# Self-attention softmax: the reciprocals of the row sums made on GpSimd instead of VectorE

## The chip, the cores and the metric

The kernel runs on one core of one Trainium2 chip, in one launch. The metric is the device time of one execution in microseconds (us). The kernel before took 3425.3 us, the median of three runs (3423.97, 3425.3 and 3429.12).

## What is computed

The input x is (4, 1024, 512) in float32. A first cross-attention block (16 heads, with a context of 64 rows) and a layer norm are followed by a transformer block: quantised self-attention (16 heads of 32 columns), quantised cross-attention, and a gated feed-forward layer with 2048 hidden columns. The change lies in the self-attention alone. Of the reference:

```python
def _fq(x, delta, zp, n_bits):
    xi = _round_ste(x / delta) + zp
    xq = jnp.clip(xi, 0.0, 2.0 ** n_bits - 1.0)
    return (xq - zp) * delta
...
sim = jnp.einsum('bhid,bhjd->bhij', _fq(q, dq, 128.0, 8), _fq(k, dk, 128.0, 8)) * SCALE
attn = jax.nn.softmax(sim, axis=-1)
out = jnp.einsum('bhij,bhjd->bhid', _fq(attn, dw, 0.0, 8), _fq(v, dv, 128.0, 8))
```

So each row of scores is exponentiated, divided by its sum times the step `dw` of the quantisation, rounded to a whole number, and multiplied with the quantised values.

## The kernel before, in words

The work is cut into 8 chunks of 512 query rows, two for each of the 4 batches. For every batch both chunks go through the first cross-attention (`cross`), then each chunk goes through self-attention (`self_attention`) and the rest (`middle`). The feed-forward steps of a chunk are not a stage of their own: `feed` deals them out, by a plan worked out from counts and not from times, into the slots of the following chunk's stages. They are the "hosted" work below. Every engine runs its own list of instructions in the order written here; semaphores join the lists.

Self-attention of a chunk has 64 units. A unit is one head for 128 query rows: scores of 128 x 1024. It runs in 70 slots, slot s issuing stages of different units:

- TensorE makes the scores of unit s (L2006, L2007) into a pair of PSUM banks. There are two such pairs, so unit s waits until ScalarE has emptied the pair of unit s-2. Then come hosted matrix multiplications (L1722 to L1724), then the eight transposes of unit s-5 (L2018) into PSUM bank 4, which is the only bank for them, and in two slots out of four half of the product with the values (L2032).
- VectorE takes the row maximum of unit s (`mx`, L1603). In even slots it next makes the reciprocals of the two units s-2 and s-1: `den` = sum times `dw` (L1609), and `rec` = 1/`den` (L1611). Then it turns the transposed weights of unit s-5 into bf16 (`w1T`, L1622), which empties bank 4, and does its hosted steps (`gate` L1514, `x` L1477).
- ScalarE scales the maximum (`nb`, L1287) and exponentiates from PSUM into `e` (L1293); the same instruction sums the row, and a second short one writes out the sum into `sum1`. There are 5 buffers `e1`: unit s waits until GpSimd has read unit s-5.
- GpSimd multiplies `e` by `rec`, adds 1024 and writes float16, which rounds the number (`w1b`, L989). It does this for unit s-2, in `scale_unit`. There are 3 buffers `w1b`: unit u waits for the transposes of unit u-3. Hosted steps on GpSimd are `u_lo` (L1008), and in the first chunk that hosts any, `fw_lo` (L996). Ahead of unit 8 it adds a bias row to the residual (`x`, L910). Elsewhere it computes `rstd`, a power with exponent -0.5 of one column (L904), for the layer norms.

The waits that the change touches are these: `wait_emptied(("s1", n, s))` says that `e` and the sum of unit s are written, `rec_ready` that the reciprocals of a pair are, `w1_ready` that GpSimd has written `w1b`, `("p1T", n, u)` filled that the transposes of unit u are done.

Of the kernel before, what the change touches and what calls it, by code (L numbers as in the profile page):

```python
# [9 lines left out]
ALU = mybir.AluOpType  # L10
# [3 lines left out]
P = 128  # L14
# [13 lines left out]
UNITS = HG * NT * 4  # L28
# [231 lines left out]
def build(nc, a, out):  # L260

    ctx = ExitStack()
    with ctx:
        def sb(name, shape, dt=F32):
            return ctx.enter_context(nc.sbuf_tensor(name, shape, dt))

        def sem(name):
            return ctx.enter_context(nc.semaphore(name))

        def signal(name, keys, by=1):  # L270
            return Signal(sem(name), keys, by)
# [24 lines left out]
        delta = sb("delta", [P, 8])  # L296
# [17 lines left out]
        nb1 = sb("nb1", [P, 4])  # L314
        sum1 = sb("sum1", [P, 8])
        den1 = sb("den1", [P, 8])
        rec1 = sb("rec1", [P, 8])
        k2 = sb("k2", [P, HG, 4 * SC], BF16)
        v2 = sb("v2", [P, PAIRS, 2 * DH], BF16)
# [70 lines left out]
        chunks = range(CHUNKS)  # L390
# [61 lines left out]
        units = [(n, u) for n in chunks for u in range(UNITS)]  # L452
        maxed1 = signal("maxed1", units)
        nb_ready = signal("nb_ready", units)
        rec_ready = signal("rec_ready", [(n, g) for n in chunks for g in range(UNITS // 2)])
        w1_ready = signal("w1_ready", units)
        e2_done = signal("e2_done", [(n, t) for n in chunks for t in range(NT)])
# [10 lines left out]
        def bank_of(key):  # L468
            return FILL[key][0]

        def bank(i):
            return psum[:, i, :]

        def wait_filled(eng, key):

            i, n = FILL[key]
            eng.wait_ge(filled[i], n + 1)

        def wait_emptied(eng, key):

            i, n = FILL[key]
            eng.wait_ge(emptied[i], n + 1)
# [389 lines left out]
        def _(pool):  # L872
            pool.memset(ident[:], 0.0).then_inc(ident_ready, 1)
            pool.memset(mhalf[:], -0.5).then_inc(ident_ready, 1)
            pool.wait_ge(ident_ready, 2)
            pool.affine_select(out=ident[:], in_=ident[:], compare_op=ALU.not_equal, fill=1.0, base=0,
                               pattern=[[-1, P]], channel_multiplier=1).then_inc(ident_ready, 1)
# [104 lines left out]

            def scale_unit(n, u):

                pool.wait_ge(rec_ready.sem, rec_ready.at((n, u // 2)))
                if u >= NH:
                    wait_filled(pool, ("p1T", n, u - NH))
                pool.sem_inc(waits_over, 1)
                pool.tensor_scalar(w1b[u % NH][:], e1[u % NE][:], rec1[:, u % 8:u % 8 + 1], HALF,  # L989
                                   ALU.mult, ALU.add).then_inc(w1_ready.sem, 1)  # L990
# [358 lines left out]
        def _(dve):  # L1349
            steps = [0]  # L1350

            def link(ins):

                steps[0] += 1
                ins.then_inc(step, 1)
                return ins

            def landed():

                dve.wait_ge(step, steps[0])  # L1360
# [14 lines left out]
            def emptied_bank(ins, key):  # L1375
                return ins.then_inc(emptied[bank_of(key)], 1)
# [220 lines left out]
            def self_attention(n):  # L1597

                for s in range(S_SLOTS):
                    if s < UNITS:  # L1600
                        wait_filled(dve, ("s1", n, s))
                        i = bank_of(("s1", n, s))
                        dve.tensor_reduce(mx1[:, s % 4:s % 4 + 1], psum[:, i:i + 2, :].rearrange("p i n -> p (i n)"),  # L1603
                                          AX, ALU.max).then_inc(maxed1.sem, 1)
                    if s >= 2 and s % 2 == 0 and s <= UNITS:
                        g = s // 2 - 1
                        at = slice(2 * (g % 4), 2 * (g % 4) + 2)
                        wait_emptied(dve, ("s1", n, 2 * g + 1))
                        link(dve.tensor_scalar(den1[:, at], sum1[:, at], delta[:, 3:4], None, ALU.mult))  # L1609
                        landed()  # L1610
                        dve.reciprocal(rec1[:, at], den1[:, at]).then_inc(rec_ready.sem, 1)  # L1611
                    u = s - LAG_T
                    if 0 <= u < UNITS:
                        key = ("p1T", n, u)
                        wait_filled(dve, key)
                        if u % 4 == 0 and u >= 8:
                            g = u // 4 - 2
                            if g % 4 == 3:
                                wait_filled(dve, ("a1", n, g // 4))
                            else:  # L1620
                                dve.wait_ge(w1T_used.sem, w1T_used.at((n, g)))
                        emptied_bank(dve.tensor_scalar(w1T[u % 8][:].rearrange("p k q -> p (k q)"),  # L1622
                                                       bank(bank_of(key)).bitcast(FP16), -HALF, W_HIGH, ALU.add, ALU.min), key)
                    hg, at = divmod(s - LAG_T - 19, 16)
                    if hg >= 0 and at == 0:
                        weighted_low(n, hg)
                    if n >= 1:
                        feed(n - 1, host_plan(n - 1), first_in_S(n) + s)
                weighted_low(n, HG - 1)
# [517 lines left out]
```

## Time and profile before

| | |
|---|---|
| median of 3 runs | 3425.3 us (3423.97 to 3429.12) |
| the profiled execution's own time | 3415.72 us |
| its span, first to last instruction | 3413.9 us |
| TensorE busy | 2951.5 us, 86% |
| VectorE busy | 2205.9 us, 65% |
| ScalarE busy | 1671.2 us, 49% |
| GpSimd busy | 1515.0 us, 44% |
| mean granted TensorE clock | 0.925 |

Busy times are sums over the span; TensorE's ends are modelled, so its share is no measure of its peak. In the page's list of groups, each row has the line, the engine, the operation with its output and inputs, its shapes and count, then the busy time, the mean duration in ns, and the idle time of the engine just before these instructions with what ended it. In the names of engines PE is TensorE, PEld its weight load, DVE VectorE, ACT ScalarE and POOL GpSimd.

### The profile page before, as it was taken

The page shows a single profiled execution, that of the slowest core. Times are in us where ns is not written, and L with a number is a line of the kernel's source. Part 1 is how long each engine was busy: PE and PEld are TensorE (multiplying, and loading weights), DVE is VectorE, ACT ScalarE, POOL GpSimd, SP SyncE. Part 2 cuts the span into 40 slices and gives each one's busy share as a digit, 9 for nine tenths or more (in the row PEclk, how much of TensorE's full clock was granted, in tenths as well). Part 3 has the DMA queues.
Part 4 walks back from the last instruction along what each step waited for, and adds up shares of the span by engine and source line. Part 5 has one row for each costly group of instructions (what it writes and reads, how often), then busy time and mean ns, then how long its engine had stood idle before and what let it go on. Part 6 is the DMA issues. An engine that isn't in the chain of part 4 may idle for free.

```text
span 3413.9 us, 50797 instructions
## 1 busy us (share of the span) xinstructions
PE 2951.5 (86%) x19712; PEld 2143.4 (63%) x19712; DVE 2205.9 (65%) x3543; ACT 1671.2 (49%) x2690; POOL 1515.0 (44%) x1182
## 2 busy tenths in 40 slices
PE   7677686887899899799889889899988989889999
PEld 6555445556677656566667656656777746656777
DVE  4456695883666596786565597687565588588521
ACT  5332572783333484574433375376333276387321
POOL 3554353663645253454455154354364154355321
PEclk9888657998999899899999999999999989999999
DMA  8653102334444213323453313313453322232444
GB/s 273 222 201 133 56 1 111 127 122 185 156 163 151 81 63 124 130 87 149 133 180 115 117 51 128 130 70 130 145 190 99 142 75 100 95 122 75 169 153 160
DMA packets 199758, 436.40 MB, mean 128 GB/s; under 512 B 94944, under 2 KB 103392, under 8 KB 182368
## 3 DMA queue, kind: packets, MB, share of 16 engines
q1 hardware_dynamic: 199520, 433.15, 35.6%
q8 instruction: 158, 2.59, 0.3%
q14 instruction: 80, 0.66, 0.1%
HBM read 363.38 MB, written 65.54 MB: 126 GB/s over the span
## 4 chain that ended last, share of the span: by engine, by line
PE 54%; DVE 24%; ACT 8%; issue 6%; POOL 4%; DMA 3%; SPq 1%; POOLq 0%; DVEq 0%; ACTq 0%
PE psum L1722 16%; PE psum L1724 14%; PE psum L1723 14%; DVE mx L1603 8%; DVE w1T L1622 4%; PE psum L2018 4%; ACT e L1293 2%; PE psum L2006 2%; DVE den L1609 2%; ACT psum L1180 2%; DVE gate L1514 1%; DMA unsplit<-in_L_xattn_ff_w 1%; ACT ht_hi L1179 1%; POOL w_lo L898 1%; PE psum L2032 1%
## 5 line engine op out<-in xcount | busy, mean ns | idle before, releaser
L989 POOL TENSOR_SCALAR w1b<-e,rec 128x1024 f16<-128x1024 f32 x512 | 574.5, 1122 | 696.3 <-DVE rec L1611 506.2
L1603 DVE TENSOR_REDUCE mx<-psum 128x1 f32<-128x1024 f32 x512 | 621.7, 1215 | 50.0 <-PE psum L2007 50.0
L1293 ACT ACTIVATE e<-psum,nb,scale 128x1024 f32<-128x1024 f32 x512 | 617.5, 1206 | 16.9
L1722 PE MATMUL psum<-h_hi,fw_hi 128*128 128x512 f32 x1024 | 463.3, 452 | 31.6 <-DVE h_lo L1379 10.0
L1723 PE MATMUL psum<-h_lo,fw_hi 128*128 128x512 f32 x1024 | 415.6, 406 | 0.0
L1724 PE MATMUL psum<-h_hi,fw_lo 128*128 128x512 f32 x1024 | 414.6, 405 | 0.0
L1622 DVE TENSOR_SCALAR w1T<-psum 128x1024 bf16<-128x1024 f16 x512 | 348.3, 680 | 92.0 <-PE psum L2018 87.2
L2018 PEld LDWEIGHTS psum<-ident,w1b 128*128 128x128 f16 x4096 | 259.8, 105 | 231.4 <-issue 192.4
L2018 PE MATMUL psum<-ident,w1b 128*128 128x128 f16 x4096 | 350.7, 234 | 61.9 <-DVE w1T L1622 58.7
L904 POOL TENSOR_TENSOR rstd<-ve,mhalf 128x1 f32<-128x1 f32 x128 | 86.9, 679 | 484.9 <-DVE ve L1485 484.9
L1477 DVE TENSOR_TENSOR x<-psum,x 128x512 f32<-128x512 f32 x224 | 152.2, 684 | 226.8 <-PE psum L1724 226.1
L1722 PEld LDWEIGHTS psum<-h_hi,fw_hi 128*128 128x128 f32 x1024 | 198.5, 194 | 152.3 <-issue 98.7
L1287 ACT ACTIVATE nb<-mx,nscale 128x1 f32<-128x1 f32 x512 | 149.8, 293 | 257.8 <-DVE mx L1603 249.1
L1722 PE MATMUL psum<-w_hi,ht_hi 128*128 128x512 f32 x640 | 257.9, 403 | 20.4 <-DVE e L1540 13.9
L1008 POOL TENSOR_TENSOR u_lo<-gate,u_hi 128x512 fp32r<-128x512 f32 x128 | 164.4, 1287 | 203.0 <-ACT u_hi L1218 197.3
L1723 PE MATMUL psum<-w_lo,ht_hi 128*128 128x512 f32 x640 | 251.7, 393 | 0.0
L1724 PE MATMUL psum<-w_hi,ht_lo 128*128 128x512 f32 x640 | 251.5, 393 | 0.0
L1722 PE MATMUL psum<-fw_hi,u_hi 128*128 128x512 f32 x512 | 226.3, 442 | 28.4 <-POOL u_lo L1008 13.7
L898 POOL TENSOR_TENSOR w_lo<-mixed,w_hi 128x512 fp32r<-128x512 f32 x140 | 190.2, 1382 | 130.8 <-ACT w_hi L1187 130.8
L1724 PEld LDWEIGHTS psum<-h_hi,fw_lo 128*128 128x128 f32 x1024 | 200.7, 196 | 46.9
L1125 ACT ACTIVATE qt<-psum,rounder,inv 128x512 f32<-128x512 f32 x128 | 99.9, 780 | 247.4 <-PE psum L1724 244.0
L2007 PE MATMUL psum<-k_odd,q_turned 32*128 32x512 bf16 x512 | 219.7, 430 | 0.0
(180 smaller groups left out, 6114.3 us busy)
## 6 DMA issues: line engine op xcount, KB each, us to landing
fw_hi<-pieces SPq DMA_DIRECT2D x168, 512.0 KB, 3.3
fw_lo<-pieces SPq DMA_DIRECT2D x168, 512.0 KB, 4.3
w_hi<-kept SPq DMA_DIRECT2D x45, 1024.0 KB, 4.9
w_lo<-kept SPq DMA_DIRECT2D x45, 1024.0 KB, 7.2
mixed<-mixed SPq DMA_DIRECT2D x32, 1024.0 KB, 5.1
fbias<-in_fside_Bx16xSxS SPq DMA_DIRECT2D x64, 256.0 KB, 3.0
unsplit<-in_L_xattn_ff_w SPq DMA_DIRECT2D x24, 512.0 KB, 5.1
pieces<-fw_hi SPq DMA_DIRECT2D x24, 512.0 KB, 2.6
```

The source lines that it names most:

```text
L898: pool.tensor_tensor(w_lo[s][:, k, :], w_mixed[s][:, k, :], w_hi[s][:, k, :].bitcast(F32), ALU.subtract).then_inc(block_lo_done.sem, 1)
L989: pool.tensor_scalar(w1b[u % NH][:], e1[u % NE][:], rec1[:, u % 8:u % 8 + 1], HALF, ALU.mult, ALU.add).then_inc(w1_ready.sem, 1)
L1008: pool.tensor_tensor(u_lo[:, m, :], gate[:, m, :], u_hi[:, m, :].bitcast(F32), ALU.subtract).then_inc(u_lo_done.sem, 1)
L1293: act.activation(e1[s % NE][:], psum[:, i:i + 2, :].rearrange("p i n -> p (i n)"), ACT.Exp, bias=nb1[:, s % 4:s % 4 + 1], scale=scale[:, 0:1],
L1477: return emptied_bank(dve.tensor_tensor(xt, bank(bank_of(key)), xt, ALU.add), key)
L1603: dve.tensor_reduce(mx1[:, s % 4:s % 4 + 1], psum[:, i:i + 2, :].rearrange("p i n -> p (i n)"), AX, ALU.max).then_inc(maxed1.sem, 1)
L1622: emptied_bank(dve.tensor_scalar(w1T[u % 8][:].rearrange("p k q -> p (k q)"), bank(bank_of(key)).bitcast(FP16), -HALF, W_HIGH, ALU.add, AL ...
L1722: pe.matmul(o, s_hi, m_hi, start=first, stop=False)
L1723: pe.matmul(o, s_hi, m_lo, start=False, stop=False)
L1724: return pe.matmul(o, s_lo, m_hi, start=False, stop=last)
L2007: ins = pe.matmul(bank(i + 1), q1_turned[turned, hg, t * P:t * P + P], k1[1][turned, hg, :], start=True, stop=True)
L2018: ins = pe.transpose(bank(bank_of(key)).bitcast(FP16)[:, k * P:k * P + P], w1b[u % NH][:, k * P:k * P + P], ident16[:])
```

## The change

The two small instructions of a pair of units leave VectorE's list. GpSimd does them at the start of `scale_unit` for the even unit: it waits until the sums of both units are written, multiplies them by `dw`, waits on its own semaphore, raises the result to the power -1 with a second operand `mone` that holds -1, waits again on its own semaphore, and scales. The odd unit of the pair has no wait on `rec_ready` any more. `mone` is filled once at the start.

```diff
+        mone = sb("mone", [P, 2])
...
+        den_ready = signal("den_ready", [(n, g) for n in chunks for g in range(UNITS // 2)])
...
             pool.memset(mhalf[:], -0.5).then_inc(ident_ready, 1)
+            pool.memset(mone[:], -1.0)
...
             def scale_unit(n, u):
 
-                pool.wait_ge(rec_ready.sem, rec_ready.at((n, u // 2)))
+                if u % 2 == 0:
+                    at = slice(u % 8, u % 8 + 2)
+                    wait_emptied(pool, ("s1", n, u + 1))
+                    pool.tensor_scalar(den1[:, at], sum1[:, at], delta[:, 3:4], None, ALU.mult).then_inc(den_ready.sem, 1)
+                    pool.wait_ge(den_ready.sem, den_ready.at((n, u // 2)))
+                    pool.tensor_tensor(rec1[:, at], den1[:, at], mone[:], ALU.pow).then_inc(rec_ready.sem, 1)
+                    pool.wait_ge(rec_ready.sem, rec_ready.at((n, u // 2)))
                 if u >= NH:
                     wait_filled(pool, ("p1T", n, u - NH))
...
-                    if s >= 2 and s % 2 == 0 and s <= UNITS:
-                        g = s // 2 - 1
-                        at = slice(2 * (g % 4), 2 * (g % 4) + 2)
-                        wait_emptied(dve, ("s1", n, 2 * g + 1))
-                        link(dve.tensor_scalar(den1[:, at], sum1[:, at], delta[:, 3:4], None, ALU.mult))
-                        landed()
-                        dve.reciprocal(rec1[:, at], den1[:, at]).then_inc(rec_ready.sem, 1)
```

On VectorE, the list before has these instructions in the middle of a chunk's self-attention; `mx` is the maximum of the unit of the slot, `w1T` belongs to the unit five earlier, and "waits" names the semaphores of an instruction:

```order
L1603 TENSOR_REDUCE mx1<-psum 128x1 [waits filled0]
L1609 TENSOR_SCALAR den1<-sum1,delta 128x2 [waits emptied2]
L1611 RECIPROCAL rec1<-den1 128x2 [waits step]
L1622 TENSOR_SCALAR w1T_1<-psum 128x1024 [waits filled4]
L1603 TENSOR_REDUCE mx1<-psum 128x1 [waits filled2]
L1622 TENSOR_SCALAR w1T_2<-psum 128x1024 [waits filled4]
```

The changed list has at the same place (its lines are numbered differently, L1612 is the maximum and L1624 is `w1T`):

```order
L1612 TENSOR_REDUCE mx1<-psum 128x1 [waits filled0]
L1624 TENSOR_SCALAR w1T_7<-psum 128x1024 [waits filled4]
L1612 TENSOR_REDUCE mx1<-psum 128x1 [waits filled2]
L1624 TENSOR_SCALAR w1T_0<-psum 128x1024 [waits w1T_used,filled4]
```

`den` and `rec` are gone there, and with them VectorE's wait on `emptied2`, that is on ScalarE's sums, which stood between a maximum and `w1T` in every second slot.

On GpSimd, the list before has two scalings for each pair of units, each with a wait on `rec_ready`, and here and there a hosted step:

```order
L989 TENSOR_SCALAR w1b<-e_3,rec 128x1024 [waits rec_ready,filled4]
L1008 TENSOR_TENSOR u_lo<-gate,u_hi 128x512 [waits u_hi_done]
L989 TENSOR_SCALAR w1b<-e_4,rec 128x1024 [waits rec_ready,filled4]
L989 TENSOR_SCALAR w1b<-e_0,rec 128x1024 [waits rec_ready,filled4]
```

The changed list has four instructions for a pair (L998 is the scaling, `filled4` is the wait for the transposes of the unit three earlier):

```order
L991 TENSOR_SCALAR den1<-sum1,delta 128x2 [waits emptied2]
L993 TENSOR_TENSOR rec1<-den1,mone 128x2 [waits den_ready]
L998 TENSOR_SCALAR w1b_2<-e1_0,rec1 128x1024 [waits rec_ready,filled4]
L998 TENSOR_SCALAR w1b_0<-e1_1,rec1 128x1024 [waits filled4]
```

The wait on ScalarE has moved to GpSimd, and two waits on GpSimd's own instructions stand ahead of the first scaling. ScalarE's and TensorE's lists keep their order.

## Rows read from the trace of the kernel before

**Rows 1.** The page's chain that ended last: share of the span by line.
```profile
PE psum L1722 16%; PE psum L1724 14%; PE psum L1723 14%; DVE mx L1603 8%; DVE w1T L1622 4%; PE psum L2018 4%; ACT e L1293 2%; PE psum L2006 2%; DVE den L1609 2%; ACT psum L1180 2%; DVE gate L1514 1%; DMA unsplit<-in_L_xattn_ff_w 1%; ACT ht_hi L1179 1%; POOL w_lo L898 1%; PE psum L2032 1%
```
**Rows 2.** Windows of four chunks' self-attention: busy (count), granted clock, DMA.
```profile
378.00:525.00 147.00, 115.57 (x1152) 67.18 (x1148) 130.21 (x195) 104.59 (x198) 76.32 (x65) 0.51 0.03 12
607.00:785.00 178.00, 158.88 (x1446) 102.76 (x1445) 147.95 (x211) 137.69 (x239) 114.87 (x85) 0.95 0.32 113
1162.00:1316.00 154.00, 137.02 (x1335) 81.24 (x1336) 137.03 (x207) 116.78 (x215) 86.58 (x73) 0.92 0.19 69
1418.00:1591.00 173.00, 158.12 (x1446) 102.31 (x1446) 141.48 (x211) 127.90 (x228) 86.56 (x73) 0.95 0.28 103
```
**Rows 3.** Chain of waits in the windows of Rows 2, in their order, by line.
```profile
by line: DVE mx L1603 26.6%; PE psum L2018 21.4%; DVE w1T L1622 19.3%; PE psum L2006 6.7%; PE psum L2032 5.8%; issue 5.3%; DVE den L1609 5.2%; ACT e L1293 3.5%; DVE rec L1611 3.0%; POOL w1b L989 2.3%; ACT nb L1287 0.8%; PE psum L2007 0.3%
by line: DVE mx L1603 12.9%; issue 12.1%; ACT e L1293 9.4%; PE psum L1722 8.7%; PE psum L2018 6.6%; DVE den L1609 6.5%; PE psum L1723 5.8%; PE psum L1724 5.8%; DVE w1T L1622 5.3%; PE psum L2006 3.9%; DMA unsplit<-in_L_xattn_ff_w 3.1%; ACT n
by line: DVE mx L1603 33.4%; DVE w1T L1622 17.3%; PE psum L1722 6.0%; DVE den L1609 5.8%; PE psum L2018 5.5%; issue 5.3%; ACT e L1293 4.3%; PE psum L2006 4.0%; PE psum L1723 3.3%; PE psum L1724 3.3%; DVE gate L1514 2.7%; DVE rec L1611 1.8%;
by line: PE psum L1722 14.0%; DVE mx L1603 13.0%; PE psum L2018 10.2%; PE psum L1723 9.6%; PE psum L1724 9.6%; issue 8.2%; PE psum L2006 6.5%; DVE w1T L1622 6.4%; ACT e L1293 5.2%; DVE den L1609 3.4%; PE psum L2032 2.9%; ACT gate L1232 2.2%
```
**Rows 4.** Groups by line of the whole span: the instructions moved, and GpSimd's nearest kin.
```profile
L1609 DVE TENSOR_SCALAR den<-sum,delta 128x2 f32<-128x2 f32 x256 | 102.5, 400 | 55.2 <-ACT e L1293 54.9
L1611 DVE RECIPROCAL rec<-den 128x2 f32<-128x2 f32 x256 | 42.4, 166 | 8.8
L989 POOL TENSOR_SCALAR w1b<-e,rec 128x1024 f16<-128x1024 f32 x512 | 574.5, 1122 | 696.3 <-DVE rec L1611 506.2 <-issue 135.1 <-PE psum L2018 50.0
L1052 POOL TENSOR_SCALAR w2b<-e 128x1024 f16<-128x1024 f32 x32 | 33.5, 1047 | 6.7 <-POOL e L1047 6.7
L916 POOL TENSOR_TENSOR x<-x,row_L_xattn_bo 128x1024 f32<-128x1024 f32 x16 | 38.3, 2394 | 0.0
L910 POOL TENSOR_TENSOR x<-x,row_L_xattn_a_bo 128x2048 f32<-128x2048 f32 x16 | 73.1, 4571 | 3.5 <-DVE z L1496 2.8
L874 POOL MEMSET mhalf<- 128x4 f32 x1 | 0.1, 103 | 0.0
```
**Rows 5.** One tile each, `den` and the power `rstd`: durations in ns, min/median/max.
```profile
L1609 DVE TENSOR_SCALAR den<-sum,delta x256: 214/228/4129, 383.0 to 3152.1; 128x2 f32<-128x2 f32 x128
L904 POOL TENSOR_TENSOR rstd<-ve,mhalf x128: 547/779/789, 184.2 to 3262.3; 128x1 f32<-128x1 f32 x128
```
**Rows 6.** Timeline of a stall: start, duration, engine, instruction.
```profile
1185.12 4.54 POOL L910 TENSOR_TENSOR x<-x,row_L_xattn_a_bo 128x2048 f32<-128x2048 f32 x1
...
1186.45 3.23 DVE L1609 TENSOR_SCALAR den<-sum,delta 128x2 f32<-128x2 f32 x1
```
**Rows 7.** Timeline of one pair of units and its transposes, third window of Rows 2.
```profile
1206.99 0.19 ACT L1293 ACTIVATION_READ_ACCUMULATOR e<-psum,nb,scale 128x1 f32 x1
1207.22 0.23 DVE L1609 TENSOR_SCALAR den<-sum,delta 128x2 f32<-128x2 f32 x1
1207.48 0.17 DVE L1611 RECIPROCAL rec<-den 128x2 f32<-128x2 f32 x1
1207.87 1.12 POOL L989 TENSOR_SCALAR w1b<-e,rec 128x1024 f16<-128x1024 f32 x1 [2.06 <-DVE rec L1611]
...
1210.45 1.12 POOL L989 TENSOR_SCALAR w1b<-e,rec 128x1024 f16<-128x1024 f32 x1
1212.53 0.61 PE L2018 MATMUL psum<-ident,w1b 128*128 128x128 f16 x8 [0.17 <-DVE w1T L1622]
1214.53 0.62 PE L2018 MATMUL psum<-ident,w1b 128*128 128x128 f16 x8
```
**Rows 8.** Timeline of `rstd` after its input, without and with VectorE's `z` beside it.
```profile
301.58 0.55 POOL L904 TENSOR_TENSOR rstd<-ve,mhalf 128x1 f32<-128x1 f32 x1 [2.79 <-DVE ve L1485]
303.15 0.54 DVE L1496 TENSOR_SCALAR z<-x,mv,rstd 128x512 f32<-128x512 f32 x1
303.31 0.78 POOL L904 TENSOR_TENSOR rstd<-ve,mhalf 128x1 f32<-128x1 f32 x1 [1.18 <-DVE ve L1485]
```

## The prediction

> **What bounds the kernel now.** I read the page's chain first: TensorE's hosted and projection products carry it, and the two instructions that move are a small part, `den` at 2% [rows 1]. So the answer can't come from whole-span shares. The change acts only in the eight self-attention stages, and I cut the span there. Of the eight, the first (378 to 525 us) and the second (607 to 785) are single cases. The third stands for the third, fifth and seventh ("even" below, 154 us each), the fourth for the fourth, sixth and eighth ("odd", 173 us each), which have the same lengths [rows 2]. The reader should see that no engine is far ahead: in the even stage TensorE and VectorE are both busy 137 of 154 us; in the odd one TensorE is busy 158 of 173 us; GpSimd is at 87 us in both, and at 115 of 178 us in the second stage, where it also splits weight pieces. The first runs at a granted clock of 0.51, TensorE's 1.2 GHz level, with TensorE busy 116 and VectorE 130 of 147 us.
>
> Then I read the chain inside each stage [rows 3]. In the first and the even ones VectorE's maximum and `w1T` lead. In the odd ones TensorE's lines do. That split decides how much a lighter VectorE is worth.
>
> **What is removed.** VectorE loses 256 `den` and 256 `rec`: 102.5 + 42.4 us busy, and 55.2 + 8.8 us idle just before them, 209 us in all [rows 4]. Not all of it is on the path. By the chains, `den` and `rec` hold 5.2 + 3.0 = 8.2% of 147 us, 12.1 us, in the first stage; 5.8 + 1.8 = 7.6% of 154 us, 11.7 us, in an even one; 3.4% of 173 us, 5.9 us, in an odd one, and up to 2.2% more for `rec`, which is not among the twelve lines shown; 6.5% of 178 us, 11.6 us, in the second, with the same remark [rows 3]. Taking 1.5% for the two shares not shown (an estimate, between 0 and their last shown lines), 12 + 14 + 3 x 11.7 + 3 x 8.5 = 87 us is the most that the removal gives, if nothing else is late.
>
> Part of it is a stall. `den` takes 214 to 228 ns but 400 on average, and up to 4129 [rows 4, 5]. The long one of [rows 6] ends at 1189.68, when GpSimd's bias addition ends at 1189.66: `den` is held until GpSimd is through. The mean says that shorter stalls of this kind are common, beside `w1b`. 256 x (400 - 225) ns = 45 us of VectorE's 209 are this. I take it that it can't come back elsewhere on VectorE: `mx`, `w1T` and the hosted steps that remain read PSUM, where `den` had SBUF alone.
>
> **What is added, on GpSimd.** Per pair of units: one `den` of two columns, a wait on its own semaphore, one power of two columns, another such wait.
> - `den` on GpSimd: no such row. Its bounds are a memset of four columns at 0.10 us and the 1024-column scaling at 1.12 [rows 4]. The additions give a fixed part: 4571 - 2394 ns for 1024 columns more leaves about 0.22 us at none. I take 0.25.
> - A wait of GpSimd on itself: `w2b` stands idle 6.7 us before 32 instructions, 0.21 us each [rows 4]. Two of them, 0.42.
> - The power: one column takes 0.55 us at the least [rows 5], and 0.78 when VectorE's `z` (SBUF to SBUF) runs beside it [rows 8]. No such instruction of VectorE runs in self-attention once `den` is gone, so 0.55 is the price of one column. For two, the low end is 0.55 again (a price per instruction), the high end near 0.22 + 2 x 0.33 = 0.88 (the fixed part once, the rest twice), the far end 1.10 (everything twice). I take 0.75, between the first two.
>
> Together 1.42 us a pair, 1.22 to 1.77 with the ends of the power, plus some 0.18 of gaps between the instructions that are not in busy time: 1.6 us.
>
> As latency this is nearly free. Now the first `w1b` of a pair starts 0.69 us after ScalarE has written the second sum (1206.99 + 0.19 to 1207.87), since VectorE comes to `den` only after its maximum; it will start some 1.5 us after. But its transposes come only at 1212.53, 3.5 us after it ends at 1208.99, and those of the second at 1214.53, 3.0 us after 1211.57 [rows 7]. A delay of 0.8 us fits. So it is GpSimd's throughput that counts: what it must do in a stage, one after another. Busy time now, plus 32 x 1.6 us, plus 6 us before the first pair of sums and after the last `w1b` (an estimate from one unit's path in [rows 7]): first stage 76.3 + 51 + 6 = 134 us against 147 now; even 86.6 + 51 + 6 = 144 against 154; odd 144 against 173; second 114.9 + 51 + 6 = 172 against 178 [rows 2].
>
> **The sum.** Each stage gives the smaller of the chain's share and what GpSimd's floor allows, less something for jitter, since a queue at 90% can't be kept full. First: 12 by the chain, 13 by the floor, taken 9. Even: 11.7 by the chain, 10 by the floor, taken 6, three times. Odd: up to 8.5 by the chain, floor far away, but TensorE at 158 of 173 is next and takes back half: 4, three times. Second: 14 by the chain, 6 by the floor, and its DMA waits remain: 1. Total 9 + 18 + 12 + 1 = 40 us. Outside self-attention nothing changes; the one memset at the start is hidden behind the first loads. The profiled execution goes from 3415.7 to about 3376 us. The median of the runs was 9.6 us above that execution, so I predict 3385 us.
>
> Two rules of the Trainium skill bear on this. On the power: the rows show 2.1 ns per column for an addition of two inputs (4571 - 2394 ns over 1024 columns). The page "GPSIMD Engine Reference", section "Elementwise — side-by-side cycle accounting", says that a GpSimd instruction has a dispatch cost in software, and a two-input body then takes about 2.6 cycles a column; by that the second column of the power is nearly free, the power takes 0.55 us, each floor falls by 6 us and the sum would be near -55 us. No row shows two columns. Against the change: the same page, section "Engine selection", advises VectorE for elementwise work because GpSimd is about twice as slow; the rows make it worse than that here, 0.55 against 0.166 us for the reciprocal. By that rule alone the time would rise, which is the last rival below; what weighs against it is that GpSimd idles 67 us in an even stage.
>
> **Rivals.**
> - *GpSimd never limits.* The power costs 0.55, TensorE and ScalarE leave room, and nearly the whole share of the chain comes back: 75 us, 3350 us. For it: GpSimd's floor in an even stage would then be 138 us. Against: TensorE is busy 137 us there, ScalarE 117 with the exponentials in series with the maxima.
> - *The time goes elsewhere.* TensorE, at 89% and 91% in the even and odd stages, is late next, and GpSimd with a power of 0.9 to 1.0 us keeps the first and second stages where they are: 10 us or less comes back, 3415 to 3425 us. For it: TensorE has half of the odd chain. Against: VectorE has over half of the even one.
> - *GpSimd becomes the bound.* One mechanism: in every pair GpSimd needs more than the stage's pair takes, falls behind, uses up the 3 us before the transposes, and from then on TensorE waits for `w1b`. With a power of 1.3 us a pair adds 2.15 us instead of 1.6, a floor 18 us higher: even 162 (+8 each), first 152 (+5), second 190 (+12), odd 162, still under 173: +41 us, 3466 us. It decides from a power of about 1.15 us on, where even 157, first 146 and second 185 cancel the odd stages' gain. For it: nothing shows the power with two columns. Against: 1.3 is more than twice the price of one.
>
> That the change doesn't do what it says is hardly open: the order of both lists shows the two instructions gone from VectorE and present on GpSimd.
>
> **How the numbers follow.** Forecast, between 25 and 60 us gained: 0.52, its own range 3365 to 3400. GpSimd never limits (60 to 85 us): 0.16. Gains of 7 to 25 us, half of the second rival: 0.10. Within 7 us of no change, its other half: 0.09. GpSimd becomes the bound: 0.13. The range goes from 3345, which takes in nearly all of the second case (87 us would be 3338), to 3425, which takes in the small gains and half of the no-change case; outside lie about 0.02 and 0.17. A change of 0.2%, 6.8 us, is about what a measurement can tell from none. Faster: 0.52 + 0.16 + 0.10 = 0.78; same 0.09; slower 0.13.
>
> **What would show it.** The power's mean duration: 0.55 to 0.9 us, else the floors are wrong. The `w1b` rows: idle on VectorE's `rec` gone, and in its place idle on ScalarE's `e`. If TensorE's weight loads of L2018 wait for `w1b` for long in the even stages, GpSimd limits. The self-attention stages should be near 138, 177, 148 and 169 us; the stages between them unchanged. VectorE's busy time should fall by 145 us, and the maximum after `e` should be waiting for TensorE's scores in the even stages. The prediction is wrong if an even stage takes over 154 us, or if the stages shrink and the time does not.

## The result, and the profile after

The changed kernel took 3403.2 us, the median of four runs (3399.72 to 3408.15), against 3425.7 us before (now of four runs too): a ratio of 0.9941, with a 95% interval of 0.9924 to 0.9959. That is a gain of 0.6%, 20 us by the ratio; timed again below, it was 0.9950. Forecast were 40 us. Both executions that were profiled are at the edges of their kernels' scatter, the one before low and this one high, so their spans differ by 7.5 us only, 3413.9 against 3406.4.

The page's chain that ended last, shares of the span by engine and by line:

```profile
PE 60%; DVE 11%; POOL 11%; ACT 7%; issue 6%; DMA 2%; SPq 1%; POOLq 0%; DVEq 0%; ACTq 0%
PE psum L1724 17%; PE psum L1726 15%; PE psum L1725 15%; PE psum L2020 5%; POOL w1b L998 3%; PE psum L2008 3%; DVE mx L1612 2%; ACT e L1302 2%; PE psum L2034 2%; ACT psum L1189 1%; DVE w1T L1624 1%; POOL u_lo L1017 1%; POOL rec L993 1%; DMA fw_lo<-pieces 1%; POOL w_lo L901 1%
```

Where VectorE's maximum had 8% and `den` 2% [rows 1], the maximum (now L1612) has 2%, and GpSimd's scaling (L998) and power (L993) are on the chain instead. The groups of the changed kernel, from the page and from its trace by line, that answer to [rows 4]:

```profile
L1612 DVE TENSOR_REDUCE mx<-psum 128x1 f32<-128x1024 f32 x512 | 623.1, 1218 | 121.2 <-PE psum L2009 121.0
L998 POOL TENSOR_SCALAR w1b<-e,rec 128x1024 f16<-128x1024 f32 x512 | 574.7, 1122 | 138.6 <-PE psum L2020 66.3
L993 POOL TENSOR_TENSOR rec<-den,mone 128x2 f32<-128x2 f32 x256 | 181.8, 710 | 21.4
L991 POOL TENSOR_SCALAR den<-sum,delta 128x2 f32<-128x2 f32 x256 | 75.5, 295 | 275.1 <-ACT e L1302 262.2
```

The power of two columns takes 710 ns (forecast 750), `den` 295 (250). The reader should see the idle times too: GpSimd's 696 us before `w1b` have become 139 there and 275 before `den`, which waits for ScalarE's sums. VectorE now waits for TensorE's scores before the maximum.

The windows of the four stages of [rows 2], in the changed kernel (TensorE, weight load, VectorE, ScalarE, GpSimd busy with counts, then clock and DMA), and the chain inside the third:

```profile
377.00:518.00 141.00, 114.54 (x1136) 66.08 (x1137) 118.73 (x131) 104.58 (x198) 108.44 (x129) 0.51 0.03 12
600.00:784.00 184.00, 161.48 (x1446) 104.19 (x1444) 128.15 (x147) 137.61 (x239) 146.95 (x149) 0.92 0.31 110
1161.00:1313.00 152.00, 138.78 (x1336) 82.40 (x1336) 125.49 (x145) 116.25 (x215) 118.72 (x137) 0.91 0.20 70
1415.00:1586.00 171.00, 156.72 (x1450) 101.98 (x1452) 127.97 (x147) 127.60 (x227) 118.70 (x137) 0.95 0.28 102
```

```profile
by line: POOL w1b L998 17.1%; issue 10.8%; PE psum L2020 10.1%; PE psum L1724 8.9%; PE psum L2008 6.8%; POOL rec L993 6.2%; POOL u_lo L1017 5.1%; PE psum L1725 5.0%; PE psum L1726 4.9%; DVE mx L1612 3.9%; ACT e L1302 3.6%; DVE w1T L1624 3.2
```

In the even stage the maximum and `w1T` led with 33% and 17% [rows 3]. Now GpSimd's scaling, power and `u_lo` lead with 28% together. The second stage got longer, 184 us against 178. GpSimd in the middle of that even stage:

```profile
1195.38 0.29 POOL L991 TENSOR_SCALAR den<-sum,delta 128x2 f32<-128x2 f32 x1
1195.76 0.71 POOL L993 TENSOR_TENSOR rec<-den,mone 128x2 f32<-128x2 f32 x1
1196.70 2.34 POOL L998 TENSOR_SCALAR w1b<-e,rec 128x1024 f16<-128x1024 f32 x2 [0.23 <-POOL rec L993]
1199.13 0.30 POOL L991 TENSOR_SCALAR den<-sum,delta 128x2 f32<-128x2 f32 x1
```

From `den` to `den` it is 3.75 us with nothing hosted between: 0.29, a gap of 0.09, 0.71, a gap of 0.23, twice 1.12 with 0.10 between, 0.09. The added part is 1.32 us with all its gaps; the forecast had 1.42, and 1.6 with gaps in its floors.

The prediction named a sign of GpSimd as a limit: TensorE's weight loads for the transposes waiting for `w1b`. In the even stage, before and then changed (us in total, times, longest):

```profile
PEld psum L2018 <- POOL w1b L989: 6.0, 15, 0.6
PEld psum L2020 <- POOL w1b L998: 13.6, 21, 2.9
```

In the changed kernel 17 of the 64 transposes of this stage start within 0.5 us of the end of their `w1b`; before, none starts sooner than 2.7 us after it. So GpSimd does limit there, part of the time.

The lengths of the self-attention stages in us, from the first maximum to the end of the last `w1T`, read from the timelines of one profile each; "even" and "odd" are means of three stages. The three even stages of one profile can differ by 4 us (146.6 to 150.6 in e1), so a difference of 1 or 2 us between two kernels in this table is within the scatter. A second profile of the kernel before (e13) has 145.6, 177.5, 153.5 and 173.0:

| kernel | first | second | even | odd | time, ratio to before (interval) |
|---|---|---|---|---|---|
| before | 145.8 | 177.4 | 153.4 | 172.1 | 3421.3 to 3424.7 in the four rounds, 1 |
| changed, built again (e1) | 140.1 | 183.4 | 148.9 | 171.0 | 3405.4, 0.9950 (0.9934 to 0.9965) |
| no inversion (e2) | 137.2 | 174.7 | 142.7 | 171.0 | 3379.3, 0.9876 (0.9857 to 0.9895) |
| both engines invert (e3) | 146.0 | 186.9 | 154.8 | 173.9 | 3441.0, 1.0060 (1.0042 to 1.0078) |
| split work (e4) | 139.0 | 176.2 | 143.4 | 171.1 | 3381.0, 0.9879 (0.9862 to 0.9896) |
| changed, bias in four (e5) | 138.3 | 186.7 | 146.9 | 171.3 | 3404.0, 0.9947 (0.9930 to 0.9963) |
| split, bias in four (e6) | 138.3 | 182.9 | 143.1 | 171.2 | 3383.7, 0.9886 (0.9868 to 0.9904) |
| changed, two powers (e7) | 151.9 | 194.4 | 164.7 | 173.5 | 3482.0, 1.0178 (1.0159 to 1.0196) |
| two reciprocals (e8) | 141.0 | 176.5 | 146.0 | 170.5 | 3381.9, 0.9882 (0.9863 to 0.9901) |
| den by columns (e9) | 144.5 | 177.1 | 150.3 | 171.8 | 3407.7, 0.9956 (0.9943 to 0.9970) |
| before, bias in four (e10) | 143.8 | 180.8 | 150.5 | 173.9 | 3421.1, 0.9990 (0.9981 to 0.9998) |
| changed, power alone (e11) | 139.6 | 183.2 | 144.6 | 171.1 | 3391.4, 0.9909 (0.9894 to 0.9925) |
| stall alone (e12) | 144.8 | 179.9 | 153.0 | 171.6 | 3420.0, 0.9997 (0.9986 to 1.0007) |
| ScalarE's den (e15) | 143.0 | 180.1 | 148.4 | 172.0 | 3402.0, 0.9935 (0.9922 to 0.9948) |

### The profile page after: what moved, and what is told of

Read it like the earlier page. It is cut to its first block, busy times and chain, and to the rows that moved or that the text cites. A ratio compares the mean times of both kernels' runs of the same rounds, so it can differ in the third digit from the quotient of the medians.

```text
span 3406.4 us, 50798 instructions
## 1 busy us (share of the span) xinstructions
PE 2956.5 (87%) x19712; PEld 2148.8 (63%) x19712; DVE 2099.8 (62%) x3031; ACT 1669.4 (49%) x2690; POOL 1772.2 (52%) x1695
## 4 chain that ended last, share of the span: by engine, by line
PE 60%; DVE 11%; POOL 11%; ACT 7%; issue 6%; DMA 2%; SPq 1%; POOLq 0%; DVEq 0%; ACTq 0%
PE psum L1724 17%; PE psum L1726 15%; PE psum L1725 15%; PE psum L2020 5%; POOL w1b L998 3%; PE psum L2008 3%; DVE mx L1612 2%; ACT e L1302 2%; PE psum L2034 2%; ACT psum L1189 1%; DVE w1T L1624 1%; POOL u_lo L1017 1%; POOL rec L993 1%; DMA fw_lo<-pieces 1%; POOL w_lo L901 1%
## 5 line engine op out<-in xcount | busy, mean ns | idle before, releaser
L1612 DVE TENSOR_REDUCE mx<-psum 128x1 f32<-128x1024 f32 x512 | 623.1, 1218 | 121.2 <-PE psum L2009 121.0
L998 POOL TENSOR_SCALAR w1b<-e,rec 128x1024 f16<-128x1024 f32 x512 | 574.7, 1122 | 138.6 <-PE psum L2020 66.3
L1624 DVE TENSOR_SCALAR w1T<-psum 128x1024 bf16<-128x1024 f16 x512 | 352.0, 687 | 176.4 <-PE psum L2020 163.6
L1017 POOL TENSOR_TENSOR u_lo<-gate,u_hi 128x512 fp32r<-128x512 f32 x128 | 164.7, 1289 | 202.6 <-ACT u_hi L1227 196.8
```

The source lines that it names most:

```text
L1017: pool.tensor_tensor(u_lo[:, m, :], gate[:, m, :], u_hi[:, m, :].bitcast(F32), ALU.subtract).then_inc(u_lo_done.sem, 1)
```

## The experiments

The first question was where the missing gain is: taken back by GpSimd's added work (theory A), or never there, since TensorE or the score banks are next (theory B). Two more came with the results: theory C, that what GpSimd does per pair counts, wherever its other work stands; and theory D, that the change wins by ending the stalls of `den` beside GpSimd. In the expectations of e9 and e12, "Theory A" beside D means that VectorE's work or its wait counts, and not the stalls. Kernels timed together ran on one chip and share the runs of the kernel before.

**e1, the changed kernel again.** 

> The changed kernel once more, timed beside the kernel before on the same chip. The change gave 0.9941 of the time before; it should stay between 0.990 and 0.997. Both theories expect its second self-attention stage (the one that also splits weight pieces on GpSimd) to be longer than before by some 6 us, as in the first trace. If that stage is back at 177 us, the 6 us were a matter of DMAs.

0.995, and the second stage at 183.4 us: both repeat.

**e2, no inversion.** From the changed kernel, GpSimd's two instructions and their waits are taken out, which leaves out the normalisation; `rec1` is filled with 1.

```diff
-            pool.memset(mone[:], -1.0)
+            pool.memset(rec1[:], 1.0)
...
-                    pool.tensor_scalar(den1[:, at], sum1[:, at], delta[:, 3:4], None, ALU.mult).then_inc(den_ready.sem, 1)
-                    pool.wait_ge(den_ready.sem, den_ready.at((n, u // 2)))
-                    pool.tensor_tensor(rec1[:, at], den1[:, at], mone[:], ALU.pow).then_inc(rec_ready.sem, 1)
-                    pool.wait_ge(rec_ready.sem, rec_ready.at((n, u // 2)))
```

> No sum is inverted at all: neither engine has den or rec, and the factor is a constant 1 written once at the start, so this leaves the normalisation out. Theory A, GpSimd's queue takes back what VectorE gives: the removal alone is worth 60 to 87 us, 3340 to 3365 us, even stages near 140 us. Theory B, TensorE or the ring of score banks is next late whatever GpSimd does: 3390 to 3405 us, even stages near 149 us, as in the changed kernel.

3379 us lies between the two: the removal alone is worth 42 us, and GpSimd's part gives 26 of them back. Theory B fails, since there was more to have than the change got (even stages 142.7 us, not 149); theory A fails in the size of the ceiling. In the even stages it is worth 10.7 us and in the odd ones 1.1, where the chain of waits, here over one odd stage (1397 to 1568 us), remains with TensorE's products:

```profile
by line: PE psum L1720 19.7%; PE psum L2016 15.0%; PE psum L1721 13.3%; PE psum L1722 13.2%; PE psum L2004 9.7%; issue 7.3%; ACT e L1298 5.1%; PE psum L2030 4.5%; DVE mx L1608 3.5%; ACT gate L1237 3.4%; DVE w1T L1620 1.6%; ACT nb L1292 1.4%
```

**e3, both engines.** GpSimd gets the change's two instructions and waits on tiles `den2` and `rec2`, ahead of the old wait.

```diff
+                if u % 2 == 0:
+                    at = slice(u % 8, u % 8 + 2)
+                    wait_emptied(pool, ("s1", n, u + 1))
+                    pool.tensor_scalar(den2[:, at], sum1[:, at], delta[:, 3:4], None, ALU.mult).then_inc(den_ready.sem, 1)
+                    pool.wait_ge(den_ready.sem, den_ready.at((n, u // 2)))
+                    pool.tensor_tensor(rec2[:, at], den2[:, at], mone[:], ALU.pow).then_inc(rec2_ready.sem, 1)
+                    pool.wait_ge(rec2_ready.sem, rec2_ready.at((n, u // 2)))
                 pool.wait_ge(rec_ready.sem, rec_ready.at((n, u // 2)))
```

> The kernel before with GpSimd's two instructions and their two waits added, their result going to a scratch tile; VectorE still makes the reciprocals that are used. Theory A: the added 1.4 to 1.5 us a pair makes the time longer than before, by 20 to 50 us, the even stages 158 to 162 us. Theory B: GpSimd has room, the time is within 10 us of before.

20 us slower, the lower edge of theory A. Half of it is in the second stage (9.5 us); the even ones have 1.4, not 5 to 8. So where VectorE sets the pace, most of GpSimd's added work hides.

**e4, split work.** VectorE inverts the bare sum, GpSimd multiplies by 1/`dw`, which the kernel has in `inv`.

```diff
-                        link(dve.tensor_scalar(den1[:, at], sum1[:, at], delta[:, 3:4], None, ALU.mult))
-                        landed()
-                        dve.reciprocal(rec1[:, at], den1[:, at]).then_inc(rec_ready.sem, 1)
+                        dve.reciprocal(den1[:, at], sum1[:, at]).then_inc(rec_ready.sem, 1)
...
-                pool.wait_ge(rec_ready.sem, rec_ready.at((n, u // 2)))
+                if u % 2 == 0:
+                    at = slice(u % 8, u % 8 + 2)
+                    pool.wait_ge(rec_ready.sem, rec_ready.at((n, u // 2)))
+                    pool.tensor_scalar(rec1[:, at], den1[:, at], inv[:, 3:4], None, ALU.mult).then_inc(scaled_ready.sem, 1)
+                    pool.wait_ge(scaled_ready.sem, scaled_ready.at((n, u // 2)))
```

> VectorE inverts the sum (one instruction of 0.17 us, no den, no step between), GpSimd multiplies the result by the inverse of the quantisation step (0.29 us and one wait on itself). Per pair GpSimd does 3.0 us instead of 3.7. Theory A: the time falls below the changed kernel's, to 3355 to 3385 us, and the second stage is not longer than before. Theory B: 3395 to 3410 us, the same as the changed kernel.

3381 us, the whole ceiling within the scatter, and the softmax is still whole: the version that beats both. GpSimd spends 2.94 us a pair there, as its timeline shows:

```profile
1198.41 0.29 POOL L989 TENSOR_SCALAR rec<-den,inv 128x2 f32<-128x2 f32 x1
1198.93 2.33 POOL L994 TENSOR_SCALAR w1b<-e,rec 128x1024 f16<-128x1024 f32 x2 [0.23 <-POOL rec L989]
1201.35 0.29 POOL L989 TENSOR_SCALAR rec<-den,inv 128x2 f32<-128x2 f32 x1
```

**e5 and e6, the bias addition in four pieces.**

```diff
...
-                    if u == 8:
-                        pool.wait_ge(z_ready.sem, z_ready.at((1, n, NT - 1)))
-                        add_bias(n, "L1_xattn_a1_bo")
+                    if u in (8, 14, 20, 26):
+                        if u == 8:
+                            pool.wait_ge(z_ready.sem, z_ready.at((1, n, NT - 1)))
+                        add_bias_quarter(n, "L1_xattn_a1_bo", (u - 8) // 6)
```

> The changed kernel with GpSimd's bias addition of 4.57 us ahead of unit 8 cut into four of some 1.3 us, ahead of units 8, 14, 20 and 26. Theory A: in the changed kernel that addition puts GpSimd 6 to 8 us behind, and at 3.75 us a pair it catches up only ten pairs later, while TensorE waits for w1b. Then the even stages fall from 147 to 151 us to 142 to 146, and the time to 3385 to 3395 us. Theory C: it is the 3.75 us a pair as such, wherever the addition stands: 3400 to 3410 us.

> The kernel in which VectorE inverts and GpSimd multiplies, with the same four pieces of the bias addition. Both theories expect a small gain over the uncut one, since GpSimd is behind there for six pairs at most: 3370 to 3380 us.

3404 us, no gain in the time: theory A's burst falls as the main cause. By the table the first and even stages are 1.8 and 2.0 us shorter than in e1 and the second 3.3 longer. In the timeline of e1's even stage GpSimd does fall behind at the addition: the first `w1b` of a pair starts 1.4 us after the second sum for the first pairs, 6.2 us after it at the fifth, and still 3.5 at the fifteenth. With four pieces it is 7.0 us at the eighth pair and 4.2 at the fifteenth. In this stretch ScalarE delivers a pair mostly every 3.4 to 4.8 us, so 3.75 us and the hosted work leave little to catch up with. e6 came out at 3384, 4 us above the range expected and no better than e4.

**e7, two powers.**

```diff
+                    pool.tensor_tensor(den2[:, at], den1[:, at], mone[:], ALU.pow)
                     pool.tensor_tensor(rec1[:, at], den1[:, at], mone[:], ALU.pow).then_inc(rec_ready.sem, 1)
```

> The changed kernel with one more power per pair, into a scratch tile, that nobody waits for: 0.71 us more GpSimd work a pair, 4.5 us in all. Theory A, from GpSimd's work per pair, the hosted work and 6 us at the ends: first stage near 153 us, even 164, second 200, odd 172: 3475 to 3490 us. Theory B, that TensorE or the score banks are the bound and GpSimd has room: within 10 us of the changed kernel.

3482 us, stages 152, 194, 165 and 174: theory A's sum holds once GpSimd is plainly the bound. The 0.71 us cost 77 us where e1's 1.32 cost 26.

**e8, two reciprocals.**

```diff
-                        link(dve.tensor_scalar(den1[:, at], sum1[:, at], delta[:, 3:4], None, ALU.mult))
+                        link(dve.reciprocal(den1[:, at], sum1[:, at]))
```

> The kernel before with den as a second reciprocal (the multiplication by the quantisation step is left out, so the weights are not the reference's). VectorE has the same two instructions a pair and the same wait, but none that is held up beside GpSimd. Theory A: the stalls, 45 us of VectorE's time, are a good part of what the change wins: 3395 to 3408 us. Rival: they are hidden behind the score banks, and the instructions themselves are what counts: 3415 to 3422 us.

3382 us, below both expectations. VectorE still does two instructions a pair and still waits for ScalarE before them, and 41 of the 42 us are there:

```profile
L1609 DVE RECIPROCAL den<-sum 128x2 f32<-128x2 f32 x256 | 41.0, 160 | 66.5 <-ACT e L1293 66.2
L1611 DVE RECIPROCAL rec<-den 128x2 f32<-128x2 f32 x256 | 42.5, 166 | 8.8
```

The rows are the groups by line of e8. No `den` there is over 167 ns, against 400 on average before [rows 4]. The kernel has 61 us less of VectorE's time than before, 45 of them stalls.

**e9, `den` by columns.**

```diff
-                        link(dve.tensor_scalar(den1[:, at], sum1[:, at], delta[:, 3:4], None, ALU.mult))
+                        for c in (2 * (g % 4), 2 * (g % 4) + 1):
+                            link(dve.tensor_scalar(den1[:, c:c + 1], sum1[:, c:c + 1], delta[:, 3:4], None, ALU.mult))
```

> The kernel before, with den as two instructions of one column each instead of one of two columns. VectorE has one instruction more a pair (0.15 us, as the one-column ve), nothing moves to GpSimd. Theory D, what the change wins on VectorE is the end of the stalls of den beside GpSimd, and a one-column form is not held up, as ve never is (153 to 155 ns): 3380 to 3392 us, and no den over 0.2 us. Theory A, it is the work taken off VectorE: 3420 to 3435 us, no faster than before.

The tile `den`, durations in ns, min/median/max:

```profile
L1610 DVE TENSOR_SCALAR den<-sum,delta x512: 201/205/217, 382.2 to 3141.3; 128x1 f32<-128x1 f32 x171
```

One column is never held up, as theory D has it: of the 512, 89 start beside a GpSimd instruction that runs on for more than 0.25 us, and none takes over 217 ns. But each takes 205 ns and not the 154 of `ve`. The time is 3408 us, between the two expectations: with one instruction more than before, and all on VectorE, it is 0.4% faster than before. That is 15 us of the 42, though no stall is left. Its mean granted clock over six runs was 0.927, that of the kernel before in the same round 0.922; an estimate below puts 9 of the 15 us beside that.

**e10, before with the bias in four.** The edit of e5 in the kernel before.

> The kernel before, with the bias addition ahead of unit 8 cut into four pieces of some 1.3 us. The one stall of 3 to 4 us a stage becomes short ones. Theory D says that the long stall is a part of the 42 us, 8 of them at 3.3 us: 3403 to 3418 us. If only the many short ones count: 3418 to 3426 us.

`den` falls from 102.5 to 86.4 us, its longest from 4.13 to 1.70 us, and the time by 2 us only, 0.9990. By the table the first and even stages are 2.0 and 2.9 us shorter, where their stalls fell by 1.8 and 2.0 us; the second and odd ones are 3.4 and 1.8 us longer. So the long stall seems to count where VectorE leads, and the cut pieces to cost as much elsewhere; with a scatter of 2 us and more this is not shown.

**e11, the power alone.** GpSimd's `den` and its wait are left out, the power reads `sum1`.

> The changed kernel without its den: GpSimd raises the bare sum to the power -1, so the factor of the quantisation step is left out. GpSimd does 3.4 us a pair instead of 3.75. Theory C, GpSimd's work per pair beyond what the pair leaves it is what takes back the gain: between the kernel with split work (3.0 us a pair, 3381 us) and the changed one (3405): 3386 to 3396 us. If it is the latency of the power alone: 3400 to 3405 us.

3391 us, in the range of theory C: GpSimd's work a pair is what costs. Without 0.38 of the 1.32 us, 14 of the 26 us come back.

**e12, the stall alone.** e2 with this in VectorE's even slots:

```diff
+                    if s >= 2 and s % 2 == 0 and s <= UNITS:
+                        at = slice((s - 2) % 8, (s - 2) % 8 + 2)
+                        link(dve.tensor_scalar(den1[:, at], inv[:, 0:2], delta[:, 3:4], None, ALU.mult))
+                        landed()
```

> The kernel without any inversion of the sums, and with one VectorE instruction of two columns per pair put back at the place of den. It reads constants, waits for nothing of the pair, and its result is not used; only w1T behind it waits until it is written. Theory D: it is held up beside GpSimd as den was, and that alone brings back most of the 42 us: 3402 to 3420 us. Theory A, that the wait on ScalarE and the second instruction matter: 3380 to 3390 us.

3420 us, nearly what before took, from one instruction a pair. Alone it takes 0.22 us; here 57 of the 256 are held up, and the mean is 450 ns. The group, and the long one in the timeline:

```profile
L1612 DVE TENSOR_SCALAR den<-inv,delta 128x2 f32<-128x2 f32 x256 | 115.3, 450 | 0.0
```

```profile
1186.74 4.54 POOL L913 TENSOR_TENSOR x<-x,row_L_xattn_a_bo 128x2048 f32<-128x2048 f32 x1
1187.90 3.40 DVE L1612 TENSOR_SCALAR den<-inv,delta 128x2 f32<-128x2 f32 x1
1191.33 0.69 DVE L1624 TENSOR_SCALAR w1T<-psum 128x1024 bf16<-128x1024 f16 x1
```

GpSimd's addition ends at 1191.28, `den` at 1191.30, and `w1T` comes after it. Nothing is inverted here and VectorE doesn't wait for ScalarE, so neither the reciprocal nor that wait made the 42 us. The stalls are some 58 us here, 13 more than before. e8 has more unstalled work of these instructions, 0.33 us a pair, and is at 3382: what sets e12 apart from it is the stalls.

**e13 and e14, a second profile of before and of split work.**

> The kernel before, one more profile. Its second self-attention stage was 177 us; the kernels that add work to GpSimd had 183 to 187 there. If that is GpSimd's work, it stays within 2 us of 177; if the stage varies by itself with the loads from HBM, it may be anywhere up to 183.

> The kernel with split work, one more profile. Its second stage was 176 us, and 183 with the bias addition cut. The same question: within 2 us of 176 if GpSimd's 3.0 us a pair fit there, up to 183 if the stage varies by itself.

The second stage was 177.5 and 176.6 us, in one run each of 3425.7 and 3378.3 us. It repeats within 0.4 us, so the 6 us more of the changed kernel are no scatter. By e2, which has 174.7, it is GpSimd's two instructions that make them, beside its 12 splits of weight pieces of 2.37 us. How they do isn't settled: e11 has 183.2 and e6 182.9 with less of that work, and e10, e12 and e15 are at 180 to 181 with none of it. The granted clock differs too: in this stage TensorE was at its 1.2 GHz level for 17 us before, 14 in e2 and 31 in e1.

**e15, ScalarE's `den`.** ScalarE multiplies after the second sum of a pair, VectorE inverts.

```diff
...
+                        if s % 2 == 1:
+                            wait_emptied(act, ("s1", n, s))
+                            pair = slice(s % 8 - 1, s % 8 + 1)
+                            act.activation(den1[:, pair], sum1[:, pair], ACT.Copy, scale=delta[:, 3:4]).then_inc(den_ready.sem, 1)
...
-                        wait_emptied(dve, ("s1", n, 2 * g + 1))
-                        link(dve.tensor_scalar(den1[:, at], sum1[:, at], delta[:, 3:4], None, ALU.mult))
-                        landed()
+                        dve.wait_ge(den_ready.sem, den_ready.at((n, g)))
```

> ScalarE multiplies the two sums by the quantisation step (one more instruction of 0.29 us a pair, with a wait on its own sums), VectorE makes the reciprocal, 0.17 us without a stall; GpSimd has nothing added. If what counts is that VectorE spends no more than 0.40 us a pair and is not held up, and ScalarE's time is free: 3378 to 3388 us. If ScalarE's time is on the path through the score banks, 256 x 0.4 us come on top: 3400 to 3430 us.

3402 us. VectorE is as well off as in e4 (a reciprocal of 162 ns, no stall), and still half the gain is gone. What e15 adds beside e4 is ScalarE's 0.30 us a pair and its wait on its own sums, so these count, some 21 us against e4. GpSimd has more room: its added work, gaps included, cost 2 us at 0.52 us a pair (e4 against e2), 12 at 0.94 (e11) and 26 at 1.32 (e1).

## Why the prediction was off

**Right:** the direction; the prices (power 0.71 for 0.75, `den` 0.29 for 0.25, 1.32 us a pair for 1.42, or for 1.6 with gaps); that latency is free and throughput counts; that the stalls are GpSimd's doing and go; the time outside self-attention unchanged (2121.0 us of the span in e1, 2114.0 and 2121.3 in two profiles of the kernel before); the second stage as the one to watch.

**The ceiling, "87 us is the most that the removal gives".** e2 measured 42 us. By the stage lengths the removal is worth 8.6 us in the first stage, 2.7 in the second, 10.7 in each even one and 1.1 in each odd one, where the chain's shares gave 12, 14, 11.7 and 8.5. So the shares were nearly right where VectorE's lines lead, and failed in the second and odd stages, where other work is nearly as late: 11 and 22 us too much. Of the terms that were added up the odd one failed most (12 us forecast, 3.5 measured), then the second (1 forecast, -6.0 measured).

**The stalls.** The prediction took them as 45 us among 209 and called the shorter ones common, beside `w1b`. They are 45 us, but only 41 of the 256 `den` took over 0.3 us. Each of the 41 ends within 0.06 us of the end of a GpSimd instruction. The eight bias additions hold 27.8 us of the 45, and 12 `w1b` hold 3.2. By stage they are 3.4 us in the first, 12.0 in the second, 4.8 in an even and 5.0 in an odd one. e8 ends them, and saves 2.3 us of work a stage; it is shorter by 4.8, 0.9, 7.4 and 1.6 us. e12 has stalls again, 4.7, 12.6, 7.8 and 5.8 us of them, and is longer than e8 by 3.8, 3.4, 7.0 and 1.1 us. So a stall costs about its length in the first and even stages, and about a quarter of it or less in the others.

Over the whole kernel, from the start of `den` to VectorE's next instruction behind the pair's reciprocals, there pass, on average over the 256 pairs, 0.593 us before, 0.512 in e9, 0.395 in e8, 0.270 in e4 and nothing in e2; the times are 3423, 3408, 3382, 3381 and 3379 us. The first 0.4 us a pair cost 3 us in all, the next 0.2 us 41, which is 0.8 us for each us of VectorE (256 x 0.198 = 51 us). e12 fits (0.624 us, 3420), e10 does not: with 0.547 us it should gain 9 us and gains 2. I read the 0.4 as what the ring of score banks and TensorE leave VectorE (that is inferred). Without a stall the two instructions stay under the 0.4, and the stalls take them over it. Work above the 0.4 costs too: e9 has no stall, 0.117 us a pair more than e8 (30 us of VectorE), and takes 26 us more.

**The granted clock,** which the prediction left out of its sum, goes with the time. Over 54 of the 55 runs of the kernel before in these rounds (the one left out recorded 0.883), 0.001 more of the mean granted clock goes with 1.9 us less. By that estimate 9 of e9's 15 us and 10 of e8's 41 go with a clock of 0.927 and 0.928 against 0.922 to 0.923 of the kernel before, and 5 to 6 of the 42 us of e2 and e4 with their 0.925. Whether the shorter VectorE work raised the clock or it differed by itself, no run here tells. e8 and e9 ran at nearly the same clock, so the 26 us between them don't hang on it.

**"Odd: TensorE takes back half: 4, three times".** It takes nearly all: 1.1 us each by e2, 1.2 in the changed kernel. 12 us were forecast, 3.5 came (against the second profile of the kernel before, e13, it would be 6). The chain of [rows 3] said so, with TensorE's lines ahead and `den` at 3.4%; a share of a line that is not the leading engine's is worth less than its length.

**"Second: 1".** It lost 6.0 us in e1: the removal was worth 2.7, GpSimd's part cost 8.7. The floor of 172 us was 11 below what was measured, though it took 1.6 us a pair for 1.32.

**"Even: 6" and "first: 9".** 4.5 and 5.7. Here the removal alone was right (10.7 and 8.6 for 11.7 and 12), and GpSimd took back 6.2 and 2.9. The floor of 144 us, 135 with the measured 1.32, took GpSimd as busy throughout. In the changed kernel's even stage its waits are these (engine and line, what it waited for, us in total, times, longest):

```profile
POOL den L991 <- ACT e L1302: 51.7, 7, 46.2
POOL w1b L998 <- POOL rec L993: 6.9, 30, 0.2
POOL w1b L998 <- PE psum L2020: 5.8, 6, 1.9
```

Without the 46.2, which is before the stage's work, 5.5 us go to waits for ScalarE's sums, 2.5 of them behind one Gelu of the hosted work (L1241), and 5.8 to transposes: at some times GpSimd has nothing to do, at others it is 6 us behind, and the first is not made up in the second. In e7, where it is plainly the bound, the same sum comes out within 2 us in three of the four kinds of stage.

Added up, 9 + 1 + 18 + 12 = 40 against 5.7 - 6.0 + 13.5 + 3.5 = 17 us in e1's stages.

**Of the rivals,** "GpSimd never limits" is refuted by e2, e7 and e11. "The time goes elsewhere" describes the odd stages. "GpSimd becomes the bound" is the mechanism of the 26 us lost, though the measured power of 0.71 us is below the 1.15 from which it was to decide; with 0.71 us more (e7) the change would have been slower than before, as that rival says, by 1.8%.

## What to carry to other kernels

Split an instruction's time into its own work and its stall before moving it: here the stalls of a small VectorE instruction beside GpSimd were most of what counted, and another form of it (a reciprocal first, or single columns) ended them without moving the work, though the single columns gave back most of the gain by their own length. A share of the chain was near the truth in the stages where its engine leads and far above it in the others; how much of it counts shows only when the instruction is shortened step by step, or put back alone. And an engine whose busy share is low over the span may have 0.5 us a pair to give and not 1.3.

## What the runs showed of the hardware

- On VectorE, a multiplication of two float32 columns from SBUF to SBUF by a per-partition scalar takes 0.22 us, and up to 4.13 beside GpSimd: 41 of 256 took over 0.3 us, and all of these ended with a GpSimd instruction, within 0.06 us. One column (201 to 217 ns) and a reciprocal of two columns (152 to 168 ns) were never held up. The Trainium skill, page "SBUF — State Buffer", section "Who interferes with whom", says that a `tensor_scalar` can use VectorE's second pair of ports, which it shares with GpSimd, and that who comes second is blocked for the whole instruction. The traces agree for two columns.
- GpSimd's power costs 0.55 us for one column and 0.71 for two, so 0.16 for the second. It is neither free nor a second full price.
- GpSimd's wait on its own instruction cost 0.08 us between `den` and the power, and 0.23 between the power and the scaling; 0.21 was taken for both.
